# The closing feed-forward network of a two-layer transformer kernel: token halves, an earlier start, the bias as a product, another finish

## Reference

```python
h = jnp.einsum('bsd,df->bsf', x, w1) + b1        # 256 -> 1024
h = float2fix(h, 8)                              # round to multiples of 2^-8
h = pwlin_gelu_basic(h, 8, 8)                    # exact GELU at 33 knots on [-4, 4], linear between, rounded
out = jnp.einsum('bsf,fd->bsd', h, w2) + b2      # 1024 -> 256
return float2fix(out, 8)                         # then x = x + out
```

## Time and profile before

| | |
|---|---|
| median of 3 runs | 961.46 us (960.75 to 961.52) |
| the profiled execution | 961.48 us |
| its span, first to last instruction | 959.6 us |
| granted PE clock, mean over the span | 0.997 |
| PE busy | 902.0 us (94% of the span) |
| DVE busy | 674.2 us (70%) |
| ACT busy | 615.8 us (64%) |
| end of DVE's last operation | 957.60 us |

### The profile page before, as it was taken

One profiled execution on the slowest core, in us unless ns is written; L12 is line 12 of the kernel. 1 busy time (PEld: TensorE's weight loads), 2 busy tenths in 40 slices (PEclk: granted clock), 3 DMA queues, 4 the chain that ended last, 5 costly groups with the idle time before them and its releaser, 6 DMA issues.

```text
span 959.6 us, 15982 instructions
## 1 busy us (share of the span) xinstructions
PE 902.0 (94%) x5514; PEld 587.4 (61%) x5514; DVE 674.2 (70%) x2153; ACT 615.8 (64%) x1681; POOL 198.3 (21%) x312
## 2 busy tenths in 40 slices
PE   6889999999999999999999999999999999999986
PEld 2555565767555565577665656567756556657744
DVE  4999882763889785474588879266488988647348
ACT  3788435972879643794578943498287964369544
POOL 3200001762000000475000000177300000047300
PEclk9999999999999999999999999999999999999999
DMA  9500100000000000000000010000000000000000
GB/s 296 192 1 2 28 0 23 2 1 1 1 1 24 3 26 23 1 2 1 0 1 13 12 28 1 23 1 2 1 0 2 17 8 1 0 1 2 1 1 22
DMA packets 14558, 18.32 MB, mean 19 GB/s; under 512 B 3088, under 2 KB 11664, under 8 KB 14480
## 3 DMA queue, kind: packets, MB, share of 16 engines
q1 hardware_dynamic: 12288, 15.40, 4.8%
q10 hardware_dynamic: 2064, 1.91, 0.7%
q0 software_dynamic: 128, 0.01, 0.0%
HBM read 15.21 MB, written 2.10 MB: 18 GB/s over the span
## 4 chain that ended last, share of the span: by engine, by line
PE 61%; DVE 22%; ACT 11%; issue 4%; POOL 1%; POOLq 0%; DVEq 0%
PE bank L1082 24%; PE bank L1097 9%; PE bank L1278 6%; PE bank L1258 5%; PE bank L1352 5%; PE bank L1194 4%; ACT ring L593 4%; DVE row_max L884 4%; PE bank L1171 2%; ACT ring L634 1%; PE bank L1210 1%; PE bank L1137 1%; ACT ring L517 1%; DVE ring L892 1%; PE bank L1324 1%
## 5 line engine op out<-in xcount | busy, mean ns | idle before, releaser
L435 POOL TENSOR_TENSOR rstd<-var_eps,minus_half 128x2 f32<-128x2 f32 x32 | 23.4, 735 | 589.2 <-DVE var_eps L798 589.2
L517 ACT ACTIVATE ring<-bank 128x512 f32<-128x512 f32 x224 | 123.4, 610 | 19.2 <-PE bank L1097 19.1
L446 POOL TENSOR_TENSOR ring<-ring,row_inv 128x256 f32<-128x256 f32 x192 | 112.1, 613 | 101.9 <-DVE row_inv L979 101.9
L1097 PE MATMUL bank<-ident_s,ring 128*128 128x128 f32 x768 | 105.3, 279 | 5.3 <-POOL ring L446 2.3
L1097 PEld LDWEIGHTS bank<-ident_s,ring 128*128 128x128 f32 x768 | 82.6, 141 | 40.2 <-issue 17.4
L634 ACT ACTIVATE ring<-ring,row_max 128x256 f32<-128x256 f32 x192 | 95.1, 497 | 17.3 <-DVE row_max L972 17.3
L593 ACT ACTIVATE ring<-bank,row_max 128x256 f32<-128x256 f32 x192 | 88.2, 492 | 4.7 <-DVE row_max L884 4.7
L972 DVE CUSTOM_DVE_ANT_0 ring<-bank,maskbias 128x256 f32<-128x256 f32 x192 | 70.7, 420 | 23.4 <-issue 23.4
L884 DVE TENSOR_REDUCE row_max<-bank 128x2 f32<-128x512 f32 x128 | 79.4, 683 | 5.9 <-PE bank L1171 5.1
L1082 PE MATMUL bank<-wgu_s,act_s 128*128 128x352 f32 x256 | 78.4, 459 | 0.0
L1082 PE MATMUL bank<-ctxT_s,wk_s 128*128 128x512 f32 x160 | 75.6, 596 | 0.7 <-DVE v L870 0.7
(11 more groups left out here) (163 smaller groups left out, 1661.3 us busy)
## 6 DMA issues: line engine op xcount, KB each, us to landing
x_s<-x SPq DMA_DIRECT2D x4, 512.0 KB, 3.9
ctxT_s<-ctxT SPq DMA_DIRECT2D x4, 512.0 KB, 3.6
w_s<-w SPq DMA_DIRECT2D x2, 1024.0 KB, 16.4
out<-act_s SPq DMA_DIRECT2D x16, 128.0 KB, 1.7
wk_s<-wk SPq DMA_DIRECT2D x1, 1024.0 KB, 13.5
wv_s<-wv SPq DMA_DIRECT2D x1, 1024.0 KB, 14.8
wq_s<-wq SPq DMA_DIRECT2D x1, 1024.0 KB, 16.4
wo_s<-wo SPq DMA_DIRECT2D x1, 1024.0 KB, 16.6
```

What stands on the lines that cost most here:

```text
L446: ins = pool.tensor_tensor(probs1[i % PRING1][:, a, :], probs1[i % PRING1][:, a, :], row_inv[:, i, a:a + 1].to_broadcast([P, SEQ]), ALU.mult)
L517: act.activation(probsT[u % TRING][:, :, :].rearrange("p a q -> p (a q)"), psum(at, key)[:], ACT.Copy).then_inc(drain(at, key), 1)
L1097: ins = pe.transpose(psum(at, key)[:, c * SEQ + a * P:c * SEQ + (a + 1) * P], tile[:, a, c * P:(c + 1) * P], ident_s[:])
```

## The change

Only the network of the last group is touched, and the tail of the second attention of that group.

- The chunks are cut in units (`CLOSING`): chunks 0 to 4 for tokens 0 to 255, the same five for tokens 256 to 511, chunks 5 and 6 for all 512 tokens, and chunk 7 in two halves. These are 14 units, handed to the banks m % 4. Both halves of chunk 7 are given bank 3.
- PE transposes the first half and makes units 0 and 1 between tiles 2 and 3 of the attention's output (`closing_first`). The other hidden products follow tile 3; the second half is transposed after unit 4.
- DVE normalizes the first half ahead of the residual of tile 2, and does the units 0 and 1 ahead of the residual of tile 3.
- The order of the steps within a unit stays. At the border of the halves (`SECOND_HALF`) unit 4 is finished before unit 5 begins.
- The GELU buffers lie in `big_v` and `big_k`.
- b2 comes in as a product of one row: a row of ones (`ones_row`, set by POOL at the start) times the row b2, as the first matmul into each of the four output banks. `("o2", t)` has a bank of its own for each tile.
- ACT rounds each output tile out of PSUM by adding the large constant; DVE subtracts the constant and adds the residual in one operation.

```diff
+
+CLOSING = [(m, 0) for m in range(5)] + [(m, 1) for m in range(5)] + [(5, None), (6, None), (7, 0), (7, 1)]
+SECOND_HALF = 5
...
 def jobs_last_layer():
 
     jobs = Jobs()
-    jobs_last_hidden(jobs)
-    jobs_last_out(jobs)
+    for h in range(HALVES):
+        jobs.add(("xT3", h), 4 + h)
+    for m, h in CLOSING:
+        jobs.add(("f", m, h), m % 4)
+    for t in range(TILES):
+        jobs.add(("o2", t), 4 + t)
     return jobs
...
+def closing_columns(h):
+
+    return slice(0, GROUP) if h is None else slice(h * GROUP // 2, (h + 1) * GROUP // 2)
...
+def closing_unit(m, h):
+
+    return max(n for n, unit in enumerate(CLOSING) if unit[0] == m and ((m, h) not in CLOSING or unit[1] == h))
...
+        ones_row = sb("ones_row", [1, P])
...
+        closing_buf = [big[:, 4 * n:4 * n + 4, :] for big in (big_v, big_k) for n in range(2)]
...
             pool.memset(gelu_bias[:, 2:3], FIX).then_inc(consts_set, 1)
-            pool.wait_ge(consts_set, 8)
+            pool.memset(ones_row[:], 1.0).then_inc(consts_set, 1)
+            pool.wait_ge(consts_set, 9)
...
+            def closing(at, g):
+
+                base = g * FC1
+
+                def buf(n, part):
+                    m, h = CLOSING[n]
+                    return closing_buf[m % GELUS][:, part, closing_columns(h)]
+
+                def evacuate(n):
+                    m, h = CLOSING[n]
+                    if m >= GELUS:
+                        act.wait_ge(y_ready, base + closing_unit(m - GELUS, h) + 1)
+                    act.wait_ge(*is_filled(at, ("f", m, h)))
+                    c = closing_columns(h)
+                    act.activation(buf(n, 0), psum(at, ("f", m, h))[:, 0:c.stop - c.start], ACT.Identity,
+                                   bias=b1_s[:, m:m + 1]).then_inc(drain(at, ("f", m, h)), 1)
+
+                def fixed(n):
+                    act.wait_ge(*is_drained(at, ("f",) + CLOSING[n]))
+                    act.activation(buf(n, 0), buf(n, 0), ACT.Identity, bias=gelu_bias[:, 2:3]).then_inc(g_fixed, 1)
+
+                def low(n):
+                    act.wait_ge(g_knot, 2 * base + 2 * n + 1)
+                    act.activation(buf(n, 3), buf(n, 2), ACT.Gelu, bias=gelu_bias[:, 0:1]).then_inc(g_low, 1)
+
+                def high(n):
+                    act.wait_ge(g_low, base + n + 1)
+                    act.activation(buf(n, 2), buf(n, 2), ACT.Gelu, bias=gelu_bias[:, 1:2]).then_inc(g_high, 1)
+
+                evacuate_xT(at, 3, 0, xnT)
+                for n in range(len(CLOSING)):
+                    if n == SECOND_HALF:
+                        evacuate_xT(at, 3, 1, xnT)
+                        low(n - 1)
+                        high(n - 1)
+                    evacuate(n)
+                    if n not in (0, SECOND_HALF):
+                        low(n - 1)
+                    fixed(n)
+                    if n not in (0, SECOND_HALF):
+                        high(n - 1)
+                low(len(CLOSING) - 1)
+                high(len(CLOSING) - 1)
+                for t in range(TILES):
+
+                    act.wait_ge(*is_filled(at, ("o2", t)))
+                    act.activation(ffn_out[:, t, :], psum(at, ("o2", t))[:, 0:DM], ACT.Identity, bias=gelu_bias[:, 2:3]).then_inc(drain(at, ("o2", t)), 1)
+
             def layer0_query(at, c):
 
...
@@ -847,6 +911,76 @@
                         dve.tensor_tensor(prev[:, 1, :], prev[:, 1, :], prev[:, 3, :], ALU.add).then_inc(g_line, 1)
                         dve.wait_ge(g_line, line + 3)
                         dve.tensor_scalar(yT[:, u, :], prev[:, 1, :], FIX, FIX, ALU.add, ALU.subtract).then_inc(y_ready, 1)
+
+            def closing(sums, at, g):
+
+                base, ln = g * FC1, g * 4 + 3
+
+                def buf(n, part):
+                    m, h = CLOSING[n]
+                    return closing_buf[m % GELUS][:, part, closing_columns(h)]
+
...
+                    dve.wait_ge(g_fixed, base + n + 1)
+                    dve.tensor_scalar(bits(buf(n, 2)), bits(buf(n, 0)), KNOT_BITS, None, ALU.bitwise_and).then_inc(g_knot, 1)
+
+                def line_part(n):
+                    dve.tensor_scalar(bits(buf(n, 1)), bits(buf(n, 0)), LINE_BITS, LINE_BASE_BITS, ALU.bitwise_and, ALU.bitwise_or).then_inc(g_knot, 1)
+
+                def difference(n):
+                    dve.wait_ge(g_high, base + n + 1)
+                    dve.tensor_tensor(buf(n, 2), buf(n, 2), buf(n, 3), ALU.subtract).then_inc(g_line, 1)
+
+                def rise(n):
+                    dve.wait_ge(g_knot, 2 * base + 2 * n + 2)
+                    dve.wait_ge(g_line, 3 * base + 3 * n + 1)
+                    dve.scalar_tensor_tensor(buf(n, 1), buf(n, 1), LINE_BASE, buf(n, 2), ALU.subtract, ALU.mult).then_inc(g_line, 1)
+
+                def value(n):
+                    m, h = CLOSING[n]
+                    dve.wait_ge(g_line, 3 * base + 3 * n + 2)
+                    dve.tensor_tensor(buf(n, 1), buf(n, 1), buf(n, 3), ALU.add).then_inc(g_line, 1)
+                    dve.wait_ge(g_line, 3 * base + 3 * n + 3)
+                    dve.tensor_scalar(yT[:, m, closing_columns(h)], buf(n, 1), FIX, FIX, ALU.add, ALU.subtract).then_inc(y_ready, 1)
+
+                def end(n):
+                    difference(n)
+                    rise(n)
+                    value(n)
+
+                def step(n):
+                    if n == SECOND_HALF:
+                        end(n - 1)
+                    if n in (0, SECOND_HALF):
+                        knots(n)
+                        line_part(n)
+                    else:
+                        difference(n - 1)
+                        knots(n)
+                        rise(n - 1)
+                        line_part(n)
+                        value(n - 1)
+
+                for t in range(2):
+                    residual_and_ln_tile(sums, "o1", t, res_b, res_b, ln)
+                ln_variance(ln, 0)
+                ln_normalize(ln, 0, res_b, xn)
+                residual_and_ln_tile(sums, "o1", 2, res_b, res_b, ln)
+                step(0)
+                step(1)
+                residual_and_ln_tile(sums, "o1", 3, res_b, res_b, ln)
+                ln_variance(ln, 1)
+                step(2)
+                ln_normalize(ln, 1, res_b, xn)
+                for n in range(3, len(CLOSING)):
+                    step(n)
+                end(len(CLOSING) - 1)
+                for t in range(TILES):
+                    dve.wait_ge(*is_drained(at, ("o2", t)))
+                    dve.scalar_tensor_tensor(res_b[:, t, :], ffn_out[:, t, :], FIX, res_b[:, t, :], ALU.subtract, ALU.add).then_inc(out_ready, 1)
 
             def output_bias(at):
 
...
+                if next_group is None:
+                    closing(at, closing_pass, g)
+                    return
...
-            fp4_and_layer1(middles[last], last, None)
-            at = closing_pass
-            gelu(at, last)
-            output_bias(at)
-            for t in range(TILES):
-                finish_tile(at, last, t)
+            fp4_and_layer1(middles[GROUPS - 1], GROUPS - 1, None)
...
-            def last_hidden(at, ln, with_layer0):
+            def closing_hidden(at, units):
+                for m, h in units:
+                    product(at, ("f", m, h), psum(at, ("f", m, h))[:, 0:GROUP if h is None else GROUP // 2],
+                            [(w1_s[:, c, m * P:(m + 1) * P], xnT[:, c, closing_columns(h)]) for c in range(KC)])
+
+            def closing_half(at, g, h):
+                pe.wait_ge(xn_ready, (g * 4 + 3) * TILES + 2 * h + 2)
+                transpose_xn(at, 3, h, xn)
+                pe.wait_ge(*is_drained(at, ("xT3", h)))
+
+            def closing_first(at, g):
+
+                closing_half(at, g, 0)
+                closing_hidden(at, CLOSING[0:2])
+
+            def closing(at, g):
+                closing_hidden(at, CLOSING[2:SECOND_HALF])
+                closing_half(at, g, 1)
+                closing_hidden(at, CLOSING[SECOND_HALF:])
+                for t in range(TILES):
+
+                    wait_free(at, ("o2", t))
+                    pe.matmul(psum(at, ("o2", t))[:, 0:DM], ones_row[:], b2_s[0:1, :], start=True, stop=False)
+                for m in range(FC1):
+                    for t in range(TILES):
+                        if t % 2 == 0:
+                            h = t // 2 if (m, 0) in CLOSING else None
+                            pe.wait_ge(y_ready, g * FC1 + CLOSING.index((m, h)) + 1)
+                        key = ("o2", t)
+                        ins = pe.matmul(psum(at, key)[:, 0:DM], yT[:, m, t * P:(t + 1) * P], w2_s[:, m, :], start=False, stop=(m == FC1 - 1))
+                        if m == FC1 - 1:
+                            ins.then_inc(fill(at, key), 1)
+
...
                 for t in range(TILES):
+                    if t == TILES - 1 and next_at is None:
+                        closing_first(closing_pass, g)
                     key = ("o1", t)
                     wait_free(at, key)
```

(38 more changed lines are left out.)

9 lines of the change are left out of this document (4 added, 5 removed).

## The result

The changed kernel takes 969.72 us in the median of 4 runs (969.01 to 970.48), the kernel before 961.13 on the same chip (960.75 to 961.52). The ratio is 1.0087, 95% interval 1.0072 to 1.0102: 8.6 us slower. The forecast was 965.9, 4.4 us slower, with a range to 967.9, and the measured median lies above that range. The direction and the place were right, the size was half of what came.

What follows compares the result with a forecast made beforehand. In the last 55 us the ACT and DVE loop and PE's strict order were taken to bound the kernel. 961.48 + 2.7 (later end behind bank 3) + 1.7 (clock) = 965.9 us, range 962.6 to 967.9.

Steps and rivals of the forecast that it cites:

- The earlier start: Start of the closing: first knots at 916.1, 9.5 us earlier than at 925.58; the gain of the change.
- What the pieces cost: ACT and DVE loop: two half units at 1.98 take 3.96 against 3.04 per chunk; last rounding 951.1, only 1.1 earlier.
- rival D: ACT and DVE loop: pieces are cheaper than counted; 963.7, or 962.0 with the clock held; chance 0.09.
- The wait that sets the end: PE, unit 13: waits for bank 3 until 942.6, then 76 instructions take 16.7 us; last tile in PSUM at 959.35.
- Rival C: End of the kernel: PE is not late, the ACT and DVE chain ends last; faster, 956.9; chance 0.07.
- The clock: PE after its gap of some 6 us: lower clock when the 76 instructions begin, costing 1.7 us.
- rival B: PE's backlog behind bank 3, but the clock held at 2.4 GHz: 964.2; chance 0.10.
- the bound of 2.9: Upper limit of the clock's price, from 8 instructions of 512 columns at the kernel's start taking 6.46 against 3.5.
- The bias row's own price: PE ahead of the output products: 8 bias instructions taken at 0.22 each, bounds 0 and 0.22, 1.8 us in all.
- The finish: After the last output product: ACT rounding 0.43, one DVE operation 0.42, handoffs 0.06; end at 960.3 against 957.60, +2.7.
- The sum: Whole kernel: 961.48 + 2.7 + 1.7 = 965.9 us, 0.46% slower.

Runs made afterwards that it cites:

- own_bank: Changed kernel with one number other: unit 13, the second half of chunk 7, gets bank 0 instead of bank 3; 961.02 us, ratio 0.9987.
- gap_filled: Changed kernel with 12 idle matmuls of 128 rows (24 instructions) in PE's gap between units 12 and 13; 965.54 us, ratio 1.0041.
- bias_128_rows: Changed kernel with the bias product over 128 rows, with 1/128 in place of the ones, instead of one row; 967.94 us, ratio 1.0061.
- gap_one_row: Changed kernel with PE's gap between units 12 and 13 filled by 12 idle products of one row (24 instructions); 971.53 us, ratio 1.0101.
- finish_only: Kernel before with only the change's last part: own output banks, one-row bias products, ACT rounding, one DVE operation per tile; 959.45 us, ratio 0.9974.
- after_again: The changed kernel, nothing altered, profiled a second time; 971.38 us.
- no_bias_rows: Changed kernel without the four bias products, so b2 is left out of the result; 966.54 us, ratio 1.0045.
- tile3_first: own_bank with the first half's transposes and units 0 and 1 put back behind tile 3 on PE; 962.64 us, ratio 1.0004.

## Why the prediction was right and where it was too small

- **The earlier start** was right: first knots forecast at 916.1, measured at 915.66. Tile 2's residual was itself 0.3 earlier in this profile (912.36 against 912.68).
- **What the pieces cost** was right: the half loop 1.98 against 2.00, bank 3 free at 942.6 against 942.88, the last rounding at 951.1 against 951.63. This refutes rival D, by which a half unit is cheaper. Of 9.9 us at the start 0.6 are left at the last rounding.
- **The wait that sets the end** was right, and own_bank shows it: the same kernel without that one wait is 8.7 us faster, of which gap_filled gives 4.2 to the clock. The 76 instructions were forecast at 16.7 us at full speed and take 17.05 in gap_filled. Rival C's 956.9 is not what own_bank gave (961.02), by C's own condition: unit 13's product had to begin by 935.3, and without the wait it begins at 937.0, so that PE is still late. My expectation of own_bank passed over that.
- **The clock** is the step that failed. The mechanism was forecast (rival B, the clock held, is refuted by its 0.50), and the term "I take 1.7, as the nearest gap gave" was mis-sized: it measured 22.46 - 17.05 = 5.4 us, in the second profile 21.3 - 17.05 = 4.2, above the bound of 2.9 taken from the start of the kernel too. In both of my rows the products after the gap had 128 rows. Here eight instructions of one row stood second in line. With 128 rows in their place the clock cost 19.1 - 17.05 = 2.05 us, so for such products 1.7 was nearly right, and 2.2 to 3.4 us came with the products of one row. These are single profiles; by the times, bias_128_rows gives back 1.8 us, or 2.5 by the ratios. That such products do not hold the clock up as those of 128 rows do is clearer in the gap: gap_one_row is 6.0 us slower than gap_filled, and no faster than the changed kernel with its gap open. The bias row's own price, which I bounded by 0 and 0.22, is 0.24 from start to start at the full clock (gap_filled, eight from 943.63 to 945.55), so it was near the bound; what I had not asked is what it does to the clock.
- **The finish** was right: 0.97 us from the last product to the last DVE operation (965.39 to 966.35) against 0.91, and finish_only shows the shorter tail, 3.0 against 5.4.
- **The sum.** Forecast 965.9, profiled 970.39, a difference of 4.5: 3.7 by the clock (5.4 instead of 1.7), 0.35 by the 76 instructions, 0.3 by bank 3, under 0.1 by the finish, and 0.2 in the store, the program's end and what lies around the span (4.04 us behind DVE's last operation where it was 3.88), with 0.1 lost in rounding.

The trace agrees with the rule cited from the Trainium skill, "PSUM — Partial Sum Buffer", section "Engine vs sequencer instructions", that matmuls start in program order: finished chunks 0 to 3 waited from 939.4 to 948.64 while PE had nothing to do for 3.5 us of it.

## What to carry to other kernels

When work is cut in pieces that share a PSUM bank, look at what stands behind the last piece in TensorE's program: one wait for a bank held up 72 instructions, and one number took 8.7 us away. Try the parts of such a change one by one, for here the finish alone was worth 2.3 us, and with the idle stretches of TensorE filled 3.6, while the early start gave back nearly all it gained in smaller pieces: even with its own bank the whole change (own_bank, ratio 0.9987) is not faster than its finish alone (0.9974). A stall of TensorE ahead of a long run of matmuls can cost the stall and the clock, 4.2 us for the latter in this kernel. Filling the stall gave that back when the idle products had 128 rows and gave nothing back when they had one.

## What the runs showed of the hardware that I had not expected

- One-row float32 products keep PE busy in the profile, but in these runs they did not keep its clock up: with 24 of them in the gap the clock fell within them (0.83 in the mean of 937.40 to 942.70); with 24 of 128 rows it stayed at 1.00.
- The clock can be at the lower level though PE is busy throughout. Two profiles of the changed kernel, after and after_again, at 24.5 to 28.5 us:

```profile
24.50:28.50 4.00, 4.00 (x28) 3.16 (x20) 3.33 (x7) 3.38 (x12) 2.35 (x1) 1.00 1.03 393
```

```profile
24.50:28.50 4.00, 4.00 (x22) 2.98 (x15) 3.01 (x6) 3.40 (x13) 2.35 (x1) 0.62 1.03 391
```

  It is the same kernel, and in the second profile tile 2's residual comes 1.84 us later (914.20 against 912.36). Of the fourteen profiles five have this stretch at 0.57 to 0.62 (after_again, bias_128_rows, no_bias_rows, finish_only, tile3_first), and in these tile 2's residual starts at 913.5 to 914.2; in the nine others it starts at 911.6 to 912.8. What decides which comes is not shown. So a difference of under 2.6 us between two single profiles says nothing here until this shift is taken off. Whether it is also what spreads the runs of one kernel (own_bank's from 959.06 to 961.30) is not shown.
